# Dealing routed tokens to the experts in units of 128 instead of 256, in an eight-layer graph and mixture-of-experts program on one core

## What is computed

```python
def _L2_ffn_ref(x, Wr, W1s, b1s, W2s, b2s, W1p, b1p, W2p, b2p):
    shared = gelu(x @ W1s + b1s) @ W2s + b2s
    rw = jax.nn.softmax(x @ Wr, axis=-1)
    topw, topi = jax.lax.top_k(rw, 2)
    topw = topw / jnp.sum(topw, axis=-1, keepdims=True)
    mask = ...                                  # the two weights, at the two experts
    h = gelu(jnp.einsum('bsd,edf->bsef', x, W1p) + b1p)
    priv = jnp.einsum('bsef,efd->bsed', h, W2p) + b2p
    return shared + jnp.einsum('bsed,bse->bsd', priv, mask)

def _L3_ffn_ref(x, Wg, bg, W1, b1, W2, b2):     # the same with relu, a gate bias and no shared expert
    ...
```

## Time and profile before

| | us |
|---|---|
| median of 3 runs | 2752.92 (2751.19 to 2754.5) |
| the profiled execution: its own time | 2749.05 |
| its span, first to last instruction | 2747.2 |
| PE busy in the span | 2235.4 (81%) |
| DVE busy | 1780.1 (65%) |
| ACT busy | 1369.2 (50%) |
| POOL busy | 1295.5 (47%) |

### The profile page before, as it was taken

The page is one execution under the profiler, slowest core; times in us unless marked ns, Lnnn a source line. Parts: engine busy times, 40 slices in busy tenths (PEclk is TensorE's granted clock), DMA queues, the critical chain, the costliest instruction groups (busy, mean ns, idle before and its releaser), DMA issues.

```text
span 2747.2 us, 40763 instructions
## 1 busy us (share of the span) xinstructions
PE 2235.4 (81%) x12080; PEld 1668.3 (61%) x12080; DVE 1780.1 (65%) x4750; ACT 1369.2 (50%) x3028; POOL 1295.5 (47%) x1203
## 2 busy tenths in 40 slices
PE   4979898999999898789704356989899999999980
PEld 2545555554555554456503246989888889898880
DVE  5999898787887666643467765764455666736122
ACT  3545546574756463665403244645555545354540
POOL 1010100000010475777757775427457667567776
PEclk9989999999999899999856578999999899999995
DMA  4010104000010214232232222445455465465762
GB/s 156 1 40 1 33 0 110 16 17 17 17 33 1 50 32 118 77 79 80 69 112 67 81 43 80 125 110 154 115 140 148 120 176 141 111 170 144 185 152 75
DMA packets 235139, 233.08 MB, mean 85 GB/s; under 512 B 60365, under 2 KB 185023, under 8 KB 234002
## 3 DMA queue, kind: packets, MB, share of 16 engines
q1 hardware_dynamic: 200626, 184.23, 22.9%
q0 software_dynamic: 34272, 46.02, 8.7%
HBM read 168.02 MB, written 68.45 MB: 86 GB/s over the span
## 4 chain that ended last, share of the span: by engine, by line
PE 21%; POOL 10%; issue 8%; DVE 6%; ACT 2%; DMA 2%; POOLq 1%; SPq 0%; DVEq 0%; ACTq 0%
PE bank L2241 19%; POOL got_room L83 4%; POOL room L2210 3%; POOL c_slots L2195 2%; POOL got_room L2210 1%; PE bank L440 1%; PE bank L2366 1%; DVE c_lane_hot L2635 1%; DMA got_room<-table_dram,own_rows 1%; DMA made<-c_made 1%; ACT weights_f L2460 1%; ACT L2460 0%; DVE c_token_hot L2638 0%; DMA c_slots<-sent,c_tokens_of_slots 0%; DVE c_tile_hot L2637 0%
## 5 line engine op out<-in xcount | busy, mean ns | idle before, releaser
L1011 POOL TENSOR_TENSOR a_rstd<-a_var,minus_half 128x4 f32<-128x4 f32 x64 | 93.7, 1464 | 833.3 <-DVE a_var L1565 826.3
L2195 POOL DMA_INDIRECT c_slots<-sent,c_tokens_of_slots x340 | 358.7, 1055 | 269.9 <-PE bank L2366 144.3
L1670 DVE TENSOR_TENSOR room<-room 128x768 f32<-128x768 f32 (+2 forms) x312 | 369.9, 1208 | 22.7 <-ACT room L1407 15.2
L2241 PE MATMUL bank<-c_slots_t,c_expert 128*128 128x256 f32 x1360 | 343.6, 398 | 30.0 <-ACT weights_f L2460 21.7
L2460 ACT ACTIVATE weights_f<-bank,c_expert 128x256 f32<-128x256 f32 x680 | 276.6, 469 | 178.5 <-PE bank L2241 178.4
L2241 PE MATMUL bank<-c_experts_w,weights_f 128*128 x2720 | 346.1, 283 | 4.0 <-ACT weights_f L2460 4.0
L2241 PEld LDWEIGHTS bank<-c_experts_w,weights_f 128*128 128x128 f32 x2720 | 337.8, 199 | 14.8 <-issue 10.3
L2241 PEld LDWEIGHTS bank<-c_slots_t,c_expert 128*128 128x128 f32 x1360 | 258.6, 200 | 68.8 <-issue 36.4
L1041 PE MATMUL bank<-a_h1p,weights_a 128*128 128x512 f32 x544 | 242.5, 595 | 0.0
L2657 DVE TENSOR_TENSOR c_made<-bank,c_expert 128x256 f32<-128x256 f32 x170 | 72.1, 424 | 263.0 <-PE bank L2241 249.4
L83 POOL DMA_INDIRECT got_room<-table_dram,own_rows x175 | 185.5, 1060 | 62.0 <-issue 62.0
(11 more groups left out here) (539 smaller groups left out, 4581.7 us busy)
## 6 DMA issues: line engine op xcount, KB each, us to landing
c_expert<-packed_dram SPq DMA_DIRECT2D x170, 322.0 KB, 3.4
made<-c_made SPq DMA_DIRECT2D x170, 128.0 KB
results_dram<-a_results SPq DMA_DIRECT2D x64, 256.0 KB
room<-results_dram SPq DMA_DIRECT2D x16, 1024.0 KB, 5.7
room<-in_adj SPq DMA_DIRECT2D x32, 256.0 KB, 5.1
sent<-c_rows_to_send SPq DMA_DIRECT2D x32, 256.0 KB, 2.7
c_slots<-sent,c_tokens_of_slots POOLq DMA_INDIRECT x340
a_adj<-in_adj SPq DMA_DIRECT2D x16, 256.0 KB, 3.0
```

What stands on the lines that cost most here:

```text
L1011: rstd.did(g_.tensor_tensor(st.rstd[:, :], st.var[:, :], env.minus_half[:, 0:GT], ALU.pow), what, k)
L1670: v.tensor_tensor((dv[:, :, 0, :], other(dv))[j], sv[:, :, 0, :], other(sv), (ALU.min, ALU.max)[j]).then_inc(sort_step, 1)
L2195: pool.indirect_dma_start(out=XS[p.r % S_BUFS][:, j, :], out_offset=None, in_=env.sent_dram[p.q], in_offset=bass.IndirectOffsetOnAxis(ap=T ...
L2241: return nc.tensor.matmul(out, lhsT=lhsT, rhs=rhs, start=start, stop=stop, skip_group_check=True)
```

## The change

Places are dealt in units of 128, and a pass is still 256 places wide.

- Each expert's share is rounded up to 128. The units that make whole pairs come first (`one`: the even part of each expert's unit count), then the odd last units of all experts (`two`), paired across experts. A batch of n tiles needs n + 4 passes: 20, 28, 28, 28, 28 and 20, together 152. Its first n - 4 passes have one expert for certain (`WHOLE_PASSES`); the last 8 of each batch, 48 in all, may have two.
- Those 48 passes fetch twice, one weight for each half (`buffers`), so that there are 200 fetches for 170. Their `raise` has eight matmuls and eight activations of 128 columns; their `lower` takes the second weight half by half; their `take` is two additions.
- There are six weight rooms (`W_BUFS`) for five; a fetch waits for the pass that used its room last.
- `route` computes with 16 parts for 8 and with a slot table of 40 or 56 units for 23 or 31 passes, and has ten more operations.
- `mark` and `list` are a little narrower (40 or 56 columns for 46 or 62).
- The planner's numbers change: `HOP` 0.25 for 0.15 (both phases), `LANDS` and some entries of `LONG`, all of `PREFER_C`, and `SHARED_AFTER`. `PREFER_A` and `LONG_A` stay.
- A semaphore of the setup is dropped: SP waits on the step counter instead.

```diff
-HOP = 0.15
+HOP = 0.25
...
-SLOT_SHIFT = 8
-SLOT = 1 << SLOT_SHIFT
-SLOT_TILES = SLOT // P
-PASSES = [(2 * n * P + EXPERTS2 * (SLOT - 1)) // SLOT for n in BATCH_TILES]
+SLOT_TILES = 2
+SLOT = SLOT_TILES * P
+ROOMY = EXPERTS2 // SLOT_TILES
+PASSES = [n + ROOMY for n in BATCH_TILES]
+WHOLE_PASSES = [n - ROOMY for n in BATCH_TILES]
+PARTS = 2 * EXPERTS2
...
-W_BUFS, S_BUFS, Y_BUFS, S_ROWS = 5, 4, 4, 4
+W_BUFS, S_BUFS, Y_BUFS, S_ROWS = 6, 4, 4, 4
...
-SHARED_AFTER = (0, 3, 6, 15, 17, 31, 40, 96)
+SHARED_AFTER = (0, 6, 9, 13, 15, 31, 39, 88)
+def fetches_of(q, n):
+    return 1 if n < WHOLE_PASSES[q] else SLOT_TILES
...
             def fetch(p):
                 sp.wait_ge(tables, p.q + 1)
-                if p.r >= W_BUFS:
-                    sp.wait_ge(taken, pass_of(p.r - W_BUFS) + 1)
-                k, layer = p.r % W_BUFS, p.q // BATCHES
-                e = sp.value_load(TE[0:1, p.q, p.n:p.n + 1], min_val=0, max_val=EXPERTS2 - 1)
-                sp.dma_start(PACK[k][:, :], env.packed_dram[bass.ds(e * P + layer * EXPERTS2 * P, P), :]).then_inc(weights_in[k], 16)
+                layer = p.q // BATCHES
+                for i, k in enumerate(buffers(p)):
+                    if p.fetch + i >= W_BUFS:
+                        sp.wait_ge(taken, fetched_for[p.fetch + i - W_BUFS].m + 1)
+                    slot = p.n * SLOT_TILES + i
+                    e = sp.value_load(TE[0:1, p.q, slot:slot + 1], min_val=0, max_val=EXPERTS2 - 1)
+                    sp.dma_start(PACK[k][:, :], env.packed_dram[bass.ds(e * P + layer * EXPERTS2 * P, P), :]).then_inc(weights_in[k], 16)
...
-                    w1 = env.w("f2_w1", c) if p.r is None else W1[p.r % W_BUFS][:, c * P:(c + 1) * P]
-                    ins = mm(U[c // 2][:, (c % 2) * SLOT:(c % 2 + 1) * SLOT], w1, x, c % 2 == 0, c % 2 == 1)
+                    firsts = [env.w("f2_w1", c)] if p.r is None else [W1[k][:, c * P:(c + 1) * P] for k in buffers(p)]
+                    n = SLOT // len(firsts)
+                    for i, w1 in enumerate(firsts):
+                        at = (c % 2) * SLOT + i * n
+                        ins = mm(U[c // 2][:, at:at + n], w1, x[:, i * n:(i + 1) * n], c % 2 == 0 and i == 0, c % 2 == 1 and i == len(firsts) - 1)
...
-                link(v.tensor_tensor(CMP[:, 0:n, :], bcast(ENDS[:, :], [P, n, EXPERTS2], 1), bcast(env.tile_id[:, 0:n], [P, n, EXPERTS2], 2), ALU.is_le))
+                link(v.tensor_tensor(CMP[:, 0:slots, :], bcast(ENDS[:, :], [P, slots, PARTS], 1), bcast(env.tile_id[:, 0:slots], [P, slots, PARTS], 2), ALU.is_le))
...
-                    ins = v.tensor_tensor(YB[p.r % Y_BUFS][:, :, :], y, bcast(B2[p.r % W_BUFS][:, :], [P, SLOT_TILES, D], 1), ALU.add)
+                    biases = [B2[k] for k in buffers(p)]
+                    n = SLOT_TILES // len(biases)
+                    for i, bias in enumerate(biases):
+                        at = slice(i * n, (i + 1) * n)
+                        ins = v.tensor_tensor(YB[p.r % Y_BUFS][:, at, :], y[:, at, :], bcast(bias[:, :], [P, n, D], 1), ALU.add)
```

More of the change, by code:

```diff
@@ L1909 @@
-    "gather": (-1661.0, 1140.0), "gather_last": (-7206.0, -4435.0), "late": (-5184.0, 2479.0), "leave": (1386.0, 2204.0), "lift": (717.0, 104.0),
-    "lift_end": (-1157.0, -3577.0), "list": (2109.0, 1445.0), "load2": (5448.0, -4855.0), "load3": (-6413.0, -2931.0), "lower": (-37.0, -33.0),
-    "mark": (1745.0, 4549.0), "mask": (-439.0, 2529.0), "mix": (3148.0, -2025.0), "project": (-53.0, 5.0), "pt": (982.0, 707.0),
-    "pull": (-230.0, -920.0), "raise": (860.0, 1046.0), "route": (2376.0, 6467.0), "rows": (-1281.0, 1035.0), "save": (1437.0, 2040.0),
@@ new lines @@
+    "edge": (-2341.0, 7725.0), "enter_end": (1795.0, 501.0), "experts": (1311.0, 1873.0), "f2_score": (4787.0, -520.0), "f2_xt": (3179.0, -3078.0),
+    "f3_score": (4688.0, 2327.0), "f3_xt": (1117.0, -3743.0), "fetch": (2733.0, 3659.0), "flip": (2093.0, 216.0), "g3_xt": (-169.0, -2169.0),
+    "gather": (-952.0, -1781.0), "gather_last": (-2635.0, 430.0), "late": (832.0, 1157.0), "leave": (-1261.0, -5526.0), "lift": (2227.0, -1840.0),
+    "lift_end": (-1526.0, -4196.0), "list": (4867.0, -1483.0), "load2": (4455.0, -231.0), "load3": (-488.0, 4907.0), "lower": (-1556.0, -4060.0),
@@ new lines @@
+    "mark": (341.0, 1784.0), "mask": (-1806.0, 2203.0), "mix": (7018.0, -563.0), "project": (3004.0, -319.0), "pt": (2795.0, 1282.0),
+    "pull": (-991.0, -471.0), "raise": (675.0, 135.0), "route": (-1968.0, 457.0), "rows": (-1397.0, 328.0), "save": (2964.0, 1323.0),
+    "settle": (2305.0, 1083.0), "settle_end": (3431.0, 7108.0), "soften": (-1613.0, 69.0), "store": (2613.0, 91.0), "sum": (-3616.0, -2405.0),
+    "take": (5235.0, 5569.0), "xt": (-1816.0, -2778.0)}
+SHARED_AFTER = (0, 6, 9, 13, 15, 31, 39, 88)
@@ L1948, in work_c @@
     passes = pass_list()
+    fetched_for = [p.m for p in passes if p.r is not None for i in range(fetches_of(p.q, p.n))]
+    last_fetch = {p.r: p.fetch + fetches_of(p.q, p.n) - 1 for p in passes if p.r is not None}
+    mixed = {p.m for p in passes if p.r is not None and fetches_of(p.q, p.n) > 1}
     m_of = {("slot", p.r) if p.r is not None else ("shared", 2 * p.group + p.half): p.m for p in passes}
@@ L2005, in work_c @@
     totals.update({n: len(passes) for n in ("raise", "lower", "take")})
-    return {(n, k): Task(rows_long(k) if n == "rows" else LONG[n], needs[n](k), LANDS.get(n, 0.0), (n, k - 1) if k else None) for n in needs for k in range(totals[n])}
+    long = lambda n, k: LONG["raise_mixed"] if n == "raise" and k in mixed else rows_long(k) if n == "rows" else LONG["fetch_two"] if n == "fetch" and passes[m_of["slot", k]].m in mixed else LONG[n]
+    return {(n, k): Task(long(n, k), needs[n](k), LANDS.get(n, 0.0), (n, k - 1) if k else None) for n in needs for k in range(totals[n])}
 def phase_c(nc, env):
@@ L2607, in route @@
[L2607 to L2610 removed]
+                one, two = slice(0, EXPERTS2), slice(EXPERTS2, PARTS)
+                link(v.tensor_scalar(NEED_I[:, one], RB[:, EXPERTS2:2 * EXPERTS2], float(P - 1), None, ALU.add))
@@ L2613, in route @@
+                link(v.tensor_tensor(before, before, chosen, ALU.add))
                 for c, which in enumerate((top.first, top.second)):
```

93 lines of the change are left out of this document (55 added, 38 removed).

## The result

The change made the program slower. Its four runs have a median of 2781.86 us (2772.43 to 2786.21) beside 2752.66 us for the kernel before, a ratio of 1.0101 (95% interval 1.0074 to 1.0128): some 28 us more, where the forecast was 39 us less.

The account below looks back on a forecast made before the run. The prediction took PE's passes to bound the kernel, with POOL full behind the fifth batch. Terms -56 - 8 + 2 + 12 + 8 + 3 = -39 us from 2749.05 gave 2710, 2714 as median; range 2680 to 2758.

Parts of the forecast that it names:

- The planner's numbers: Lists of both phases: new numbers only reorder instructions; a better or worse order could not be priced, taken as 0.
- the first phase's list gets worse: Rival: the larger step reorders the first phase; 2774 at a 60 us loss; chance 0.14 for all slower cases.
- 15 passes at 3.73 us: Second phase, first five batches: 15 fewer passes save PE 3.73 us each, -56 us.
- Six pulls at the end: Sixth batch, behind the fifth batch's end: three fewer passes save POOL six pulls of 1.31 us, -8 us.
- Late weights: Passes with two experts in five batches: the second weight lands late and PE waits, 0 to 30 us, taken as +12.
- The route: Six routes, each 3.2 us longer net, 19 us at most; mostly hidden by the batch before's passes, +8 us.
- Raise in halves: PE in passes of two experts: 16 instructions of 128 columns for 8 of 256, +2 us.
- Activations in halves: ACT in raises of two experts: 2.3 us for 1.6, hidden by PE, 0.
- the first batch: Its three saved passes run beside the chain to the second routing; 3 of 11.2 us lost, +3, bounds 0 and 11.
- The second list: Second phase's new list: PE idles 54 us, a better list could win a third, a worse lose it; taken as 0.
- POOL is the limit: Rival: POOL already sets the pace, only dropped pulls count, 2737; chance 0.12 shared with weights late but some gain left.
- Late weights everywhere: Rival: all five batches pay 6 us for weights, routing shows whole, 2738 to 2754; chance 0.08 for no change.

Follow-up runs that it names:

- the doubled operations: the first kernel with eight of the route's table operations run twice in each of six routes, list unchanged: 2761.53 us, ratio 1.0035.
- the first kernel: The changed kernel with the step put back to 0.15 in the first phase's list alone: 2742.02 us, 0.9962 of the kernel before.
- the run with one fetch: the first kernel with one weight fetched for both halves of each pass and one room a pass: 2740.52 us, ratio 0.9946.
- the run with light passes: The kernel before, lists unchanged, with most of TensorE's products left out in the fourth to sixth pass of each batch: 2751.45 us, ratio 0.9990.

## Why the prediction was wrong, step by step

- **The planner's numbers, taken as 0.** This step failed first, and by itself it turns the sign: +42.2 us in the first phase. The rival "the first phase's list gets worse" stood in the prediction with its place, and its mark, a phase end moved by more than 10 us, is what the trace shows; the chance of 0.14 for all slower cases was too small. The direction was wrong too: I let sort steps pass other work, and it is the sort that falls back, with its own copies on ScalarE. Ranks have no part in it. Written out with the planner's code, the list with ranks by either step is the same; it follows the times at which the plan takes tasks to be ready, which 0.1 us a handover moves. So the argument that preferences of thousands drown the step was right of ranks and missed the thing that counts.
- **15 passes at 3.73 us, -56.** This step failed next. The work did go (60.6 us of PE), but the runs show a kink: 18 passes' products added cost 41 and 46 us, most of them taken away gave 3 to 9, with half their pulls 10.5. PE busy 94 to 96% of a stretch says that slower PE costs; it does not say that faster PE gains. Most of the gain was lost to waits (29.2 of an estimated 39.6 us in the kernel before), a part to the granted clock, which the prediction left out: it took 3.73 us a pass at 2.4 GHz, and the stretch with less work was granted 0.93 for 0.95. That the plan had packed PE, POOL and the layers' own chains to about equal length, so that the next limit lies directly behind, is argued and not shown. Whole passes left out also free ScalarE, VectorE and stores, which no run here took away, so 10.5 may be below what 18 whole passes are worth.
- **Six pulls at the end, -8.** Measured about 1: the tail is 149.3 us for 150.6, since six pulls less are issued but POOL is behind by four of them at its start.
- **Late weights, +12 of 0 to 30.** The wait came at passes of two experts, as argued (seven of its eight places), 0.8 to 4.3 us each and 17.9 in all, but not five times in each of five batches: up to the fifth batch's last take it is 7.0, nearly all of it in the fifth batch. The price of all of it was 1.5, not clear of the noise. The mechanism was right, the term mis-sized.
- **The route, +8 of 19.** By the slope of the doubled operations, 0.86 x 19 = 16. I judged most of it hidden by passes of the batch before; it is not, and it is the part of this phase that answers in both directions.
- **Raise in halves, +2.** Confirmed: 1.79 us for 1.73.
- **Activations in halves, 0, and the first batch, +3.** Not tried alone. PE's wait for hidden values in the third and fourth stage is 13.0 us in 15 places and was 6.7 in 7, so the halves are not wholly hidden.
- **The second list, 0.** With the dealing it was made for it gives 16.4, nearly the third of 54 us of idle time that I named as a bound.

The sum again, from runs: passes and pulls -10.5, route +16, second weights +1.5, together +7; measured for the dealing with the old numbers, +6.9. That the three were measured in different lists, in which a hundredth of a step moves 18 us, makes so close an agreement partly luck. The new second list then gives -16.4 and the first list +39.8, which with +6.9 is by construction the 30 us between the medians 2781.9 and 2751.5.

Rivals: "POOL is the limit" gave 2737 and the first kernel has 2742, but for another reason, as fewer pulls alone are worth 4 us. "Late weights everywhere" falls with the run with one fetch.

**Open.** What does set the second phase's pace when PE and POOL have less to do. Counted from the second phase's start, the lane sums before each route kept their times within 2 us in the run with light passes (with half the pulls too, the last four came 6.5 to 10.9 us earlier), and shorter routes moved the end, so the chain from route to route is the candidate; no run took work out of the layers between them. No run held the granted clock fixed either, so its share in the small gains is an estimate. And which way the plan's ready times put the layers ahead of the sort is read from the two windows, not tried by itself.

The version to keep is the new dealing with the old step in the first list and the table made after the list: 2731.3 us, 0.9918 of the kernel before.

## What to carry to other kernels

A number that a list-writing plan shares between phases is part of every phase: before judging a change in one, compare the order of instructions in those it doesn't touch. In a packed schedule the price of more work on the busiest engine and the gain from less are two different numbers, so measure the second by leaving work out with the list held fixed. And a wait with a large total can be worth nothing: only the run that removes it tells.

## What the runs showed that I had not expected

Taking 30.7 us off an engine that is busy 94 to 96% of 956 us shortened them by 1.5, and adding 45.5 lengthened them by 49.4. With less work TensorE was granted a lower clock, and the rest of its work took longer. One hundredth of a microsecond in a planner's step, which no instruction ever sees, moved the program by 18 us. And the time of one and the same kernel goes with the clock: three executions of the first kernel take 2732.8 to 2733.9 us at a mean granted clock of 0.893 or 0.894, five take 2741.9 to 2744.4 at 0.886 to 0.892. Which of the two brings the other about no run shows.
